# A four-layer graph kernel: how layer 2 makes and turns its transition halves, and where GpSimd takes the low half of x

## What is computed

```python
def _L2_gnn_ref(X, A, Wv, bv, aw, ab, Wk, bk):
    Xw = X @ Wv + bv
    sj, si = Xw @ aw[:d, 0], Xw @ aw[d:, 0]
    e = leaky_relu(sj[:, None, :] + si[:, :, None] + ab[0], negative_slope=0.2)
    alpha = A * exp(e)
    transition = alpha / (sum(alpha, axis=-1, keepdims=True) + 1e-12)
    H, Xk = 0, X
    for k in range(3):
        H = H + Xk @ Wk[k] + bk[k]
        Xk = transition @ Xk
    return relu(H)
x = _layernorm(x + _L2_gnn_ref(x, adj, ...))
```

## Time and profile before

| | us |
|---|---|
| median of 3 runs (lowest to highest) | 670.11 (669.84 to 670.38) |
| profiled execution, its own time | 670.04 |
| its span | 668.2 |
| PE busy in the span | 623.1 (93%) |
| DVE busy | 560.8 (84%) |
| ACT busy | 526.6 (79%) |
| POOL busy | 376.5 (56%) |

### The profile page before, as it was taken

One profiled execution on the slowest core, in us unless ns is written; L12 is line 12 of the kernel. 1 busy time (PEld: TensorE's weight loads), 2 busy tenths in 40 slices (PEclk: granted clock), 3 DMA queues, 4 the chain that ended last, 5 costly groups with the idle time before them and its releaser, 6 DMA issues.

```text
span 668.2 us, 15857 instructions
## 1 busy us (share of the span) xinstructions
PE 623.1 (93%) x5014; PEld 452.0 (68%) x5014; DVE 560.8 (84%) x1712; ACT 526.6 (79%) x1191; POOL 376.5 (56%) x448
## 2 busy tenths in 40 slices
PE   5989999999999999898999979999999997999993
PEld 4667777777777776565666646666666664778882
DVE  3889998888888888778999888988988987688886
ACT  4667888877777777868999788787877785899995
POOL 1234556665555557756777435353535353899983
PEclk9999999999999999998999999999999998999998
DMA  9591338354646433344655334545453443487773
GB/s 271 182 233 48 80 65 221 79 145 82 149 87 150 86 65 63 63 81 89 103 110 98 63 75 85 111 81 109 83 110 83 103 87 64 81 188 188 180 188 127
DMA packets 174466, 76.14 MB, mean 114 GB/s; under 512 B 122160, under 2 KB 173872, under 8 KB 174384
## 3 DMA queue, kind: packets, MB, share of 16 engines
q1 hardware_dynamic: 164208, 66.34, 42.3%
q0 software_dynamic: 8448, 8.39, 8.5%
q10 hardware_dynamic: 1728, 0.40, 0.3%
HBM read 28.97 MB, written 8.39 MB: 56 GB/s over the span
## 4 chain that ended last, share of the span: by engine, by line
PE 30%; DVE 8%; POOL 6%; DMA 6%; ACT 3%; issue 2%; SPq 0%; ACTq 0%; POOLq 0%; DVEq 0%
PE banks L86 9%; PE banks L88 8%; PE banks L87 8%; DMA xT_lo<-x_halves 3%; DMA l_TT_lo<-l_T_lo 3%; DVE l_st L1057 2%; POOL x_halves L1143 2%; POOL l_rstd L1082 2%; PE banks L1237 2%; POOL l_U L2048 1%; PE banks L1605 1%; POOL l_T_lo L1845 1%; ACT l_t L1658 1%; DVE l_u L1762 1%; DVE l_rsum L1768 1%
## 5 line engine op out<-in xcount | busy, mean ns | idle before, releaser
L1091 ACT ACTIVATE x_resident<-l_pre,l_nmr,l_rstd 128x256 f32<-128x256 f32 x256 | 140.8, 605 | 7.7 <-POOL l_nmr L1085 7.7
L983 POOL TENSOR_TENSOR hq<-hq 128x512 f32<-128x512 f32 x48 | 71.7, 1493 | 90.9 <-ACT hq L690 88.6
L1143 POOL TENSOR_TENSOR x_halves<-x_resident,x_halves 128x1024 f16<-128x1024 f32 x46 | 98.1, 2133 | 16.5 <-DVE l_pre L1339 9.9
L1057 DVE BATCH_NORM_STATS2 l_st<-l_pre 128x6 f32<-128x256 f32 x256 | 93.3, 410 | 0.0
L86 PE MATMUL banks<-Wk_lo,xT_hi 128*128 128x512 f16 (+1 forms) x256 | 83.4, 326 | 3.3 <-DVE l_pre L1339 1.8
L87 PE MATMUL banks<-Wk_hi,xT_lo 128*128 128x512 f16 (+1 forms) x256 | 83.3, 325 | 0.0
L88 PE MATMUL banks<-Wk_hi,xT_hi 128*128 128x512 f16 (+1 forms) x256 | 83.2, 325 | 0.0
L1082 POOL TENSOR_TENSOR l_rstd<-l_veps,minus_half 128x4 f32<-128x4 f32 x64 | 71.7, 1121 | 15.1 <-DVE l_veps L1071 11.2
L86 PE MATMUL banks<-W2T_lo,h_hi 128*128 128x257 f16 x256 | 70.2, 274 | 3.5 <-DVE h_lo L849 1.3
L88 PE MATMUL banks<-W2T_hi,h_hi 128*128 128x257 f16 x256 | 70.1, 274 | 0.0
L87 PE MATMUL banks<-W2T_hi,h_lo 128*128 128x257 f16 x256 | 70.1, 274 | 0.0
(11 more groups left out here) (200 smaller groups left out, 1904.8 us busy)
## 6 DMA issues: line engine op xcount, KB each, us to landing
adj<-in_adj SPq DMA_DIRECT2D x32, 256.0 KB, 3.5
x_halves<-in_x SPq DMA_DIRECT2D x16, 512.0 KB, 4.3
x_resident<-b_half SPq DMA_DIRECT2D x8, 1024.0 KB, 7.9
x_resident<-in_x POOLq DMA_DIRECT2D x16, 512.0 KB, 5.9
out<-x_resident SPq DMA_DIRECT2D x15, 512.0 KB, 3.2
x_resident<-in_L_gnn_W SPq DMA_DIRECT2D x2, 512.0 KB, 5.5
x_resident<-in_L_gnn_Wk SPq DMA_DIRECT2D x1, 768.0 KB, 9.6
xT_hi<-x_halves SPq DMA_TRANSPOSE x48, 3.2
```

Source lines behind the costliest of these rows:

```text
L983: pool.tensor_tensor(hq[:, 0, :], hq[:, 0, :], hq[:, h, :], ALU.add).then_inc(hqs_ok, 1)
L1057: dve.bn_stats(L.st[p][:, j, :], L.pre[p][:, j, :]).then_inc(L.st_ok, 1)
L1091: act.activation(K.x[:, gcols(g, j)], L.pre[p][:, j, :], ACT.Identity, bias=L.nmr[p][:, j:j + 1], scale=L.rstd[p][:, j:j + 1]).then_inc(L. ...
L1143: pool.tensor_tensor(F.xs[p][1], x_group(K, g), F.xs[p][0], ALU.subtract).then_inc(F.x_lo, 1)
```

## The change

T is no longer made in float32 first. ACT writes the high half of T graph by graph from u, with rinv as the scale of the activation (four instructions of 128x128); DVE, no longer POOL, writes the low half by four `scalar_tensor_tensor` (u times rinv, minus the high half). The two halves lie in one tile, and one DMA of 1024 columns turns both. In DVE's order the four stand behind residual 0 and 1 of the step, and norm_variance moves behind far_low 2 and 3. In POOL's order T_low is gone and norm_scales moves one step later, so that it comes behind the next x_low. T of group 0 gets its low half in DVE's step -1, behind the last step of layer 1.

```diff
--- before.py
+++ after.py
@@ -23,7 +23,7 @@
 SEAMS_PE = ('nonn', 'onononono', 'oon')
 SEAMS_ACT = ('nnononn', 'nononono', 'ooonnnonn')
 SEAMS_DVE = ('oononn', 'onono', 'nonn')
-SEAMS_POOL = ('nonno', 'onno', 'ooonnn')
+SEAMS_POOL = ('nonno', 'onno', 'oooonnn')
 
 W_SCALE = 64.0
 SQ_SCALE = 0.5
@@ -1503,18 +1503,17 @@
     adjn, adj_in = K.adjn, K.adj_in
     before_l2 = 8 * G
     rsum, reps, rinv = sb("rsum", [128, GP]), sb("reps", [128, GP]), sb("rinv", [128, GP])
-    tf = sb("tf", [128, C])
 
     def halves(name, shape):
         return [sb(f"{name}_{s}", shape, F16) for s in ("hi", "lo")]
 
-    ts, tT = halves("T", [128, C]), [halves(f"TT{p}", [128, GP, N]) for p in range(2)]
+    both, turn = sb("T", [128, 2 * C], F16), [sb(f"TT{p}", [128, 2 * GP, N], F16) for p in range(2)]
+    ts, tT = [both[:, 0:C], both[:, C:2 * C]], [[t[:, 0:GP, :], t[:, GP:2 * GP, :]] for t in turn]
     mid = [halves(f"mid{j}", [128, D]) for j in range(GP)]
 
     far = [halves(f"far{p}", [128, GP, D + 2]) for p in range(2)]
     hr = sb("hr", [128, GP, D])
-    rsum_ok, reps_ok, rinv_ok, tf_ok, t_hi, t_lo = map(
-        sem, ("rsum_ok", "reps_ok", "rinv_ok", "tf_ok", "t_hi", "t_lo"))
+    rsum_ok, reps_ok, rinv_ok, t_hi, t_lo = map(sem, ("rsum_ok", "reps_ok", "rinv_ok", "t_hi", "t_lo"))
     tT_in = [sem(f"tT_in{p}") for p in range(2)]
     far_ps, far_hi, far_lo, near_ps, mid_ps, mid_hi, mid_lo, out_ps, hr_ok = map(
         sem, ("far_ps", "far_hi", "far_lo", "near_ps", "mid_ps", "mid_hi", "mid_lo", "out_ps", "hr_ok"))
@@ -1526,7 +1525,7 @@
 
     def turned(eng, g, p):
 
-        eng.wait_ge(tT_in[p], 16 * (g - p) + 32)
+        eng.wait_ge(tT_in[p], 8 * (g - p) + 16)
 
     def sync(sp):
         def next_adj(g, p):
@@ -1535,11 +1534,11 @@
                 load_adj(K, sp, g, p)
 
         def transpose_T(g, p):
-            for s in range(2):
-                sp.wait_ge((t_hi, t_lo)[s], upto(g, 1, 1))
-                if s == 0 and reused(g):
-                    sp.wait_ge(out_ps, upto(g - 2, GP, GP))
-                sp.dma_start(tT[p][s][:], ts[s][:], transpose=True).then_inc(tT_in[p], 16)
+            sp.wait_ge(t_hi, upto(g, GP, GP))
+            sp.wait_ge(t_lo, upto(g, GP, GP))
+            if reused(g):
+                sp.wait_ge(out_ps, upto(g - 2, GP, GP))
+            sp.dma_start(turn[p][:], both[:], transpose=True).then_inc(tT_in[p], 16)
 
         def step(g, p, has):
             if has(0):
@@ -1690,10 +1689,12 @@
             act.activation(mid[j][0][:], b_near[j][:, 0:D], ACT.Copy).then_inc(mid_hi, 1)
 
         def T_high(g, p):
-            act.wait_ge(tf_ok, upto(g, 1, 1))
+            act.wait_ge(rinv_ok, upto(g, 1, 1))
             if reused(g, 1):
                 turned(act, g - 1, 1 - p)
-            act.activation(ts[0][:], tf[:], ACT.Copy).then_inc(t_hi, 1)
+            for j in range(GP):
+                act.activation(ts[0][:, j * N:(j + 1) * N], S.u[:, j * N:(j + 1) * N], ACT.Copy,
+                               scale=rinv[:, j:j + 1]).then_inc(t_hi, 1)
 
         def exponentials(g):
             act.wait_ge(S.t_ok, upto(g, GP, GP))
@@ -1758,7 +1759,8 @@
             dve.wait_ge(S.e_ok, upto(g, 1, 1))
             dve.wait_ge(adj_in[p], before_l2 + 8 * (g - p) + 16)
             if reused(g, 1):
-                dve.wait_ge(tf_ok, upto(g - 1, 1, 1))
+                dve.wait_ge(t_hi, upto(g - 1, GP, GP))
+                dve.wait_ge(t_lo, upto(g - 1, GP, GP))
             dve.tensor_tensor(S.u[:], S.e[:], adjn[p][:].rearrange("p g n -> p (g n)"),
                               ALU.mult).then_inc(S.u_ok, 1)
 
@@ -1771,14 +1773,14 @@
             dve.wait_ge(reps_ok, upto(g, 1, 1))
             dve.reciprocal(rinv[:], reps[:]).then_inc(rinv_ok, 1)
 
-        def normalised(g):
-            u = S.u[:].rearrange("p (g n) -> p g n", g=GP)
-            dve.wait_ge(rinv_ok, upto(g, 1, 1))
-            if reused(g, 1):
-                dve.wait_ge(t_hi, upto(g - 1, 1, 1))
-                dve.wait_ge(t_lo, upto(g - 1, 1, 1))
-            dve.tensor_tensor(tf[:].rearrange("p (g n) -> p g n", g=GP), u,
-                              rinv[:, :, None].to_broadcast([128, GP, N]), ALU.mult).then_inc(tf_ok, 1)
+        def T_low(g, p):
+            if reused(g, 1):
+                turned(dve, g - 1, 1 - p)
+            for j in range(GP):
+                dve.wait_ge(t_hi, upto(g, GP, j + 1))
+                c = slice(j * N, (j + 1) * N)
+                dve.scalar_tensor_tensor(ts[1][:, c], S.u[:, c], rinv[:, j:j + 1], ts[0][:, c], ALU.mult,
+                                         ALU.subtract).then_inc(t_lo, 1)
 
         def far_low(g, p, j):
             dve.wait_ge(far_hi, upto(g, GP, j + 1))
@@ -1795,8 +1797,6 @@
 
         def step(g, p, has):
             q = 1 - p
-            if has(-1):
-                norm_variance(L, dve, g - 1, q, EPS)
             if g == -3:
                 far_low(0, 0, 0)
                 far_low(0, 0, 1)
@@ -1805,6 +1805,8 @@
             if has(1) and g >= 0:
                 far_low(g + 1, q, 2)
                 far_low(g + 1, q, 3)
+            if has(-1):
+                norm_variance(L, dve, g - 1, q, EPS)
             if has(0):
                 mid_low(g, 0)
                 mid_low(g, 1)
@@ -1816,14 +1818,17 @@
             if g == -2:
                 transition(0, 0)
                 row_sums(0)
-                normalised(0)
+            if g == -1:
+                T_low(0, 0)
             if has(1) and g >= 0:
                 transition(g + 1, q)
                 row_sums(g + 1)
-                normalised(g + 1)
             if has(0):
                 residual(g, p, 0)
                 residual(g, p, 1)
+            if has(1) and g >= 0:
+                T_low(g + 1, q)
+            if has(0):
                 norm_row(L, dve, g, p, 0)
                 add_bk(g, 3)
                 norm_row(L, dve, g, p, 1)
@@ -1838,21 +1843,13 @@
         return step, 3, 1
 
     def gpsimd(pool):
-        def T_low(g, p):
-            pool.wait_ge(t_hi, upto(g, 1, 1))
-            if reused(g, 1):
-                turned(pool, g - 1, 1 - p)
-            pool.tensor_tensor(ts[1][:], tf[:], ts[0][:], ALU.subtract).then_inc(t_lo, 1)
-
         def step(g, p, has):
             q = 1 - p
             if halves_due(F, g + 2):
                 x_low(K, F, pool, g + 2, p)
-            if has(1):
-                T_low(g + 1, q)
-            if has(0):
-                norm_scales(K, L, pool, g, p)
-        return step, 2, 0
+            if has(-1):
+                norm_scales(K, L, pool, g - 1, q)
+        return step, 2, 1
 
     return sync, tensor, scalar, vector, gpsimd
 
```

## The result

The changed kernel takes 697.11 us in the median of four runs (694.74 to 700.93), the kernel before 670.25 (669.84 to 672.71) beside it: 1.0398 times as long [1.0343, 1.0453], 26.9 us more. The prediction was 695.0, with a range of 688 to 703. The profiled execution of the changed kernel took 696.14 us, with a span of 694.2 against 668.2.

A forecast was written before the change was run, and what follows sets the result against it. PE was taken as the bound, DVE close behind. Fourteen steps of 12.77 us against 155.95 gave +22.8, start +0.5, end +1.4: +24.7 on the profiled 670.04, forecast 695 us, range 688 to 703.

The forecast's parts named there:

- x_low early on POOL: Layer 2 steps: x_low starts 0.07 us after x_high, lasts 2.13, holds DVE's residuals; far_low 0 ends 1.88 us later.
- T_low at 0.26: On DVE, each of the four new T_low instructions takes 0.26 us, 1.05 for four.
- The chain behind it: On DVE, far_low 0 starts 4 x 0.334 us after the next statistic; PE is 1.88 late, steps 12.77.
- T_high in four: On ACT, four pieces take 1.14 us together against 0.63 for the single one, and delay nothing.
- One DMA: One transpose of 1024 columns lands about 3.1 us after issue, hidden from PE; with the slowest landing 0.4 late.
- norm_variance and the factors at nothing: Moved later on DVE and POOL, priced at nothing, covered by the gap before ACT uses the factors.
- Start, +0.5: Start of layer 2: the first T lands at 391.4 instead of 390.92; +0.5 us, or +2 with a slow landing.
- End, +1.4: After spread 15, PE has no project_far left and waits for T: 10.7 us against 9.28, +1.4.
- What a quicker T could give back, 3.5 us: In layer 2's 14 steps, 3.5 us over 14 x 10.89, mostly PE waiting for T's low half (2.8).
- reps held too: Rival: POOL's x_low also holds reps on DVE, residual 0 starts 0.43 us later, 701 us; chance 0.2.
- DVE holds POOL off: Rival: DVE's residuals and T_low make POOL wait instead, near 669.5 us, no change; chance 0.05.
- Faster: Rival: x_low and the residuals never meet, or meet under cover; T and far_low on time, 667 us; chance 0.07.

The follow-up runs named there:

- The half x_low: Changed kernel, but in layer 2 GpSimd subtracts the low half of x for only two of a group's four graphs; 682.32 us, 1.0191.
- POOL's order alone: Kernel before, with x_low and the earlier group's row factors ahead of T_low on POOL, T as it was; 675.02 us, 1.0082.
- T's part with POOL's old order: Changed kernel with the row factors back in their own step on POOL, norm_variance still late on DVE; 675.06 us, 1.0095.
- T alone: Changed kernel with both the row factors on POOL and norm_variance on DVE back in their old places; 671.92 us, 1.0032.
- the last kernel: T alone plus far_low 0 before residual 2, group 0's T_low before layer 1's last statistics, group 2's x_high behind the far halves; 667.67 us, 0.9971.

## Why the prediction held, point by point

**x_low early on POOL: right, in place and price.** It said 0.07 us after x_high and 2.13 long; it is 0.08 and 2.13. The half x_low shows that the hold is the cause: the time follows x_low's length. residual 0 and 1 should be over some 0.6 us behind POOL; they end at 475.87, 0.61 after. The Trainium skill (SBUF — State Buffer, Who interferes with whom) says that a DVE instruction with two SBUF inputs contends with a GpSimd instruction that reads SBUF, and that issue order decides who blocks; the trace agrees: held instructions end about their own length behind POOL's end, 0.28 us for 256 columns (both held residuals of POOL's order alone) and 0.54 for the 512 of u.

**T_low at 0.26: right.** Four take 1.13 with the tail, from 475.80 to the next statistic at 476.85 in 1.05, the sum's figure. **The chain behind it: right.** far_low 0 was put 4 x 0.334 after that statistic, at 478.19 here; it starts at 478.17. PE's wait is 1.71 on average and 1.9 at most for the 1.88 forecast, and the step 12.75 for 12.77.

**T_high in four:** mis-sized, 1.28 us for 1.14, without effect: it ends at 474.79, 1.01 before T_low starts.

**One DMA: right.** It is issued at 476.99, lands 3.0 us later, and PE waits for it in no step between spread 1 and spread 15.

**norm_variance and the factors at nothing:** right for this kernel. x_high starts 2.85 us after the spread in both. But the experiment of T's part with POOL's old order shows a price that nothing in the sum held: there the late variance pushes x_low into u. In the run with T alone, where norm_variance is in its old place, x_low ends at 460.54 and u starts at 460.60, unheld. With x_low early, no work of POOL that PE needs stands behind the variance, and its lateness costs nothing.

**Start, +0.5: the term that failed.** By the waits it was right: from spread 0 to the walk over the first T it is 13.48 us after (388.92 - 375.44) and 12.97 before (390.97 - 378.00), +0.51. The term left out PE's granted clock, which fell from 1.00 to 0.50 at about 386.7, behind PE's idle of 1.95 us and ahead of the one of 1.71 (its rows stand in the last section), and stayed there until about 393.5. From the walk's start to spread 1 it is 2.53 us instead of 1.32, with 0.50 granted, and the next step is 1.21 longer than the regular 12.75. That is 2.4 us more than forecast.

**End, +1.4: right in sum, by other parts.** The walk came 1.44 later. PE's wait for T, named as the cause, fell from 1.59 to 0.98; the wait for l_hr of graph 3, behind the held residuals on DVE, grew from 0.62 to 2.67. The two differences make +1.44. What follows the last walk, +1.62, was not forecast: the stretch of layer 3's start has a granted clock of 0.59 in 6 us, where the kernel before has 0.84 from 566 to 572. The granted clock there is 0.50 from 588.1 to 594.9, and from 564.6 to 567.9 before. T alone, the other kernel with some 6.8 us at 0.50 there, takes 112.45 us from the last walk to the end; the kernels with half of that take 110.5 to 111.3.

**The sum.** Its three terms measure 1.72 + 23.78 + 1.44 = 26.94 us where it said 24.7. What it had nothing for, -2.56 ahead of layer 2 and +1.62 behind it, makes -0.94 together: that the span's +26.0 lies closer to the forecast than 26.94 is luck.

**What a quicker T could give back, 3.5 us:** in part misread. Of the four waits for T in the earlier trace rows, 2.8 us, the longest, 1.59, stands behind spread 15; the three inside the fourteen steps make 1.2. T alone took back 1.64 us in thirteen steps.

**The rivals.** *reps held too* falls: reps starts 0.04 us ahead of x_low and lasts its plain 0.17. *DVE holds POOL off* falls: x_low keeps its 2.13. *Faster* is near what the change becomes without the early x_low and with three orders mended: 667.67 us against its 667. But its 10.89 in every step was not reached: the last kernel's thirteen steps take 11.01 on average.

Why is the whole dearer than its parts? POOL's order alone costs 0.4 us a step, since T_low on POOL still keeps x_low behind residuals 0 to 2. T alone saves 0.12. There the row factors still stand ahead of the next x_low, and it is over before u starts. So each part alone leaves something of POOL's in front of x_low. Together they leave nothing but x_high, and the step pays 1.61.

## What to carry to other kernels

Before an instruction on GpSimd is moved earlier, list what DVE does in the stretch that it will then cover: here each DVE instruction with two SBUF inputs that came to stand there waited for the whole of it, and all behind it on DVE, whatever slack GpSimd had. A move that fills an idle engine can leave the one that sets the pace waiting. And at a layer's start, price PE's idles not by their length alone: here the matmuls behind them ran at half the clock, while in the kernel before nearly as much idle time at the same place cost no clock.

## What the runs showed that was not expected

The granted clock of PE. In the changed kernel PE idles 1.95 us until 386.18, works for 1.0, and idles 1.71. The clock falls while it works between the two:

```profile
386.18:386.65 0.47, 0.47 (x5) 0.42 (x6) 0.47 (x2) 0.33 (x2) 0.47 (x1) 1.00 0.00 0
386.75:387.20 0.45, 0.45 (x3) 0.00 (x0) 0.21 (x1) 0.00 (x0) 0.45 (x1) 0.50 0.77 156
```

In the row from 388.90 to 392.40 it is still 0.50, the 1.2 GHz level; the 256-column matmuls there are 0.21 us apart, and 0.11 in the walk ahead of spread 2. In the kernel before PE idles nearly as long at the same place, 1.85 us until 387.04, then 0.70 and 0.94, 3.49 in all against 3.66, and keeps 2.4 GHz:

```profile
384.80:393.00 8.20, 4.71 (x37) 2.88 (x36) 6.44 (x19) 6.32 (x19) 4.84 (x6) 1.00 0.40 68
```

With the idle of 1.95 and no wait for T, in the last kernel, the granted clock was still 0.76 from 384 to 391 us. With idles of 1.95 and 1.91, in the kernel with half of x_low, it was 1.00 from 385.50 to 390.90, through both, and 0.50 only from there to 394.30. So the length of the idles alone does not tell what they cost. What does stays open, and each of these rows is of a single execution.

And which engine gets the memory between two POOL instructions. In the kernel with POOL's order alone, residual 2 waits for T_low (over at 465.46), gets in ahead of x_low, and ends at 465.74; x_low, issued back to back, takes 2.31 us instead of 2.13. The other regular steps of that run read the same. As the times read, a waiting DVE instruction is let in at the seam between two POOL instructions, at a cost of 0.18 to POOL, while in the middle of one it is not.
